# Another order of the calls on VectorE, GpSimd, ScalarE and TensorE in a two-layer recurrent block on one core

## The chip, the core and the metric

The kernel runs on one core of a Trainium2 chip, in one launch. The metric is the device time in microseconds (us). Every array is in HBM before the start and the output is there at the end.

## The reference

The input is 4 sequences of 1024 tokens with 256 channels, float32. Two layers follow each other, each with a sequence mixer and a feed-forward block; behind each of the four comes a residual sum and a layer norm.

```
x_conv = causal_depthwise_conv(x, 4 taps)                  # layer 0, mixer
r, i   = sigmoid(x_conv @ Wr.T + br), sigmoid(x_conv @ Wi.T + bi)
a      = sigmoid(log_a) ** (8 r);  b = sqrt(max(1 - a*a, 1e-6)) * (i * x_conv)
h      = scan along the tokens with a, b, its log clipped at -80
y0     = rmsnorm(h @ out_w.T) * norm_w
ffn    = relu(x @ W1 + b1) @ W2 + b2                       # 256 -> 1024 -> 256, in both layers
xz     = x @ in_proj.T;  xc = silu(conv4(x_in))            # layer 1, mixer (16 states per channel)
B, C, dt = parts of xc @ x_proj.T;  dt = softplus(dt * dt_w + dt_b)
h_n    = exp(dt * A_n) * h_n + dt * B_n * xc,  n = 0..15
y1     = (sum_n h_n * C_n) * silu(z) @ out_proj.T
```

## The kernel before

The 4096 tokens are cut into ten chunks (256, 256, 512 tokens; then 512 four times; 512, 384, 128), numbered 0 to 9. Channels lie on the partitions in two halves, so a full chunk is a tile of 128 x 1024. The chunks go through a software pipeline with five roles: in step i, `ahead` is chunk i+1 (its first convolution), `gate` chunk i (layer 0 mixer, first half of its feed-forward), `prep` chunk i-1 (rest of that feed-forward, input projection and convolution of layer 1), `scan` chunk i-2 (the 16 states) and `tail` chunk i-3 (output projection and feed-forward of layer 1). Each engine has its own list of calls for a step, in four variants: `opening` (steps -1 to 1), `entry` (steps 2 and 3), `step` (4 to 9) and `closing` (10 to 12). A list is written out, one call after the other, and an engine runs it strictly in this order; semaphores make it wait for the others. Nothing else sets the order. A chunk "closes" when it ends its sequence (2, 4, 6, 9) and "opens" when it begins one (0, 3, 5, 7).

The calls that the text speaks of, with the engine and the line of the profile:

- States of layer 1, for each n: TensorE spreads B and C over the partitions (`spread_B`, `spread_C`, L2037); ScalarE makes the decay (`state_decay`, L819); VectorE makes `state_input` (L1435, u times B in PSUM), two `state_scan` (L1450, one for each half; the old states come in as `carry` in chunks that don't open) and `state_output` (L1461, h times C in PSUM); GpSimd adds it up (`sum_states`, L385) and copies the last column (`save_carry`, L392), in chunks that don't close. A scan of state n waits for the copy of state n-2. TensorE's `spread_C(n)` waits for the first scan of n.
- Layer 0 mixer: TensorE `gate_mm` (L1907), ScalarE `gate_tanh`, `root_ln`, `root_exp`, VectorE `log_A` (L1356), `decay_steps` (L1362), `gate_input` (L1373), `scaled_input` (L1380) and `recurrence` (two scans, L1388, both operands in SBUF); then TensorE `out_proj0` (L1914, out_w), which waits for the recurrence and, since it shares PSUM with z, for both `z_silu` (L1406).
- Convolution of layer 1: ScalarE `mconv_tap` 1 to 3 (L781), each followed by GpSimd's `mconv_add` (L358); then VectorE `mconv_silu` (L1411).
- `dt_x` (L1423, VectorE, two operands in SBUF) makes u for the next chunk. `readout` (L1468) ends the states of `tail`. `row_stats` and `row_moments` (L1271, L1276) feed the layer norm of `gate`.

The wait of the two scans on the operand just written stands in `state_scan`:

```
dve.wait_ge(S["dBx_ready"], NS * c + n + 1)      # by state_input(n), same engine
dve.wait_ge(S["dA_ready"], UNITS * c + k + 1)
```

Of the kernel before, what the change touches and what calls it, by code (L numbers as in the profile page):

```python
# [95 lines left out]
def build(nc, xT, x, par, ffb, rows, gateT, outT, inT, xpT, opT, w1a, w2a, w1b, w2b, out):  # L96
    ctx = ExitStack()
    with ctx:
# [197 lines left out]
        def _(pool):  # L296
# [97 lines left out]
            def opening(ahead, gate, prep, scan, tail):  # L394
                if prep is not None:
                    row_scales(LN_PREP, prep)
                if gate is not None:
                    inv_rms(gate)
                    rms_residual(gate)
                    gate_scales(gate)  # L400
                    add_bias(LN_GATE, 0, x1, x1b, S["x1b_ready"], gate)
                if prep is not None:
                    save_carry(prep, 0)
                    save_carry(prep, 1)
                if ahead is not None:
                    conv_add(ahead, 1)
                if prep is not None:
                    sum_states(prep, 1)
                    save_carry(prep, 2)
                if ahead is not None:  # L410
                    conv_add(ahead, 2)
                if prep is not None:
                    sum_states(prep, 2)
                if ahead is not None:
                    conv_add(ahead, 3)
                if prep is not None:
                    save_carry(prep, 3)
# [3 lines left out]
            def entry(ahead, gate, prep, scan, tail):  # L421
# [3 lines left out]
                if tail is not None:  # L425
                    sum_states(tail, NS - 1)
                if prep is not None:
                    row_scales(LN_PREP, prep)
                if scan is not None:
                    if scan.i > 0:  # L430
                        save_carry(scan, 1)
                        sum_states(scan, 1)
                        save_carry(scan, 2)
                if tail is not None:
                    row_scales(LN_Y, tail)
                if scan is not None:
                    if scan.i > 0:
                        sum_states(scan, 2)
                        save_carry(scan, 3)
# [4 lines left out]
                if prep is not None:  # L444
                    mconv_add(prep, 1)
                    mconv_add(prep, 2)
# [3 lines left out]
                if prep is not None:  # L450
                    mconv_add(prep, 3)
                if scan is not None:
                    sum_states(scan, 6)
                if gate is not None:
                    inv_rms(gate)
                if scan is not None:
                    save_carry(scan, 6)
                    save_carry(scan, 7)
                if gate is not None:
                    rms_residual(gate)  # L460
                if scan is not None:
                    save_carry(scan, 8)
                    save_carry(scan, 9)
                    sum_states(scan, 7)
                if gate is not None:
                    gate_scales(gate)
                if scan is not None:
                    save_carry(scan, 10)
                    sum_states(scan, 8)
                    save_carry(scan, 11)  # L470
                if tail is not None:
                    add_bias(LN_Y, 1, x3, x3b, S["x3b_ready"], tail)
                if scan is not None:
# [2030 lines left out]
```

## Time and profile before

| | us |
|---|---|
| median of 3 runs (lowest to highest) | 961.77 (959.21 to 962.63) |
| the profiled execution | 961.2 |
| its span, first to last instruction | 959.4 |
| VectorE busy in it | 802.2 |
| TensorE busy | 796.9 |
| ScalarE busy | 671.6 |
| GpSimd busy | 561.4 |

The busy times are read against the span; the 1.8 us between span and time lie around it. Shares over the whole run hide that the pipeline fills and drains, so the stretches have to be read one by one.

### The profile page before, as it was taken

Reading aid. Unit: us, or ns where it says so; the run is one execution under the profiler, and the core shown is the slowest. Engines: PE = TensorE matmul, PEld = TensorE weight load, DVE = VectorE, ACT = ScalarE, POOL = GpSimd, SP = SyncE. Lnnn points to the kernel's source line nnn. Section 1 sums busy time; section 2 is a strip of 40 time slices with the busy share of each in tenths; the row PEclk is TensorE's granted clock in tenths of the full one; section 3 lists DMA queues with packets and bytes.
Section 4 is the critical chain, followed back from the end, with each engine's and each line's share of the span. In section 5 each row is a group of like instructions: output and inputs, shape, how many; then the busy total and the mean of one; then the engine's idle time right before and its main releaser. Section 6 shows DMA issues by size and latency. Waiting matters only on the chain. (4 is left out here: it accounts for less than half of the span.)

```text
span 959.4 us, 9608 instructions
## 1 busy us (share of the span) xinstructions
PE 796.9 (83%) x2802; PEld 528.2 (55%) x2802; DVE 802.2 (84%) x1013; ACT 671.6 (70%) x1345; POOL 561.4 (59%) x468
## 2 busy tenths in 40 slices
PE   2385867978987799999899999998998797787585
PEld 1264644736554556475647564756476546546464
DVE  5245566677799999999999999999999999989761
ACT  4347687588767865997699769876976685465452
POOL 0202457437836793789378937893776376565421
PEclk9597977989998889999999999999999799789597
DMA  9000000000100010001000100010000000000000
GB/s 315 12 23 22 23 1 22 1 1 0 56 1 0 1 42 13 0 1 59 8 1 1 60 1 0 1 46 0 1 1 27 1 1 1 23 0 1 22 1 22
DMA packets 10341, 19.49 MB, mean 20 GB/s; under 512 B 1457, under 2 KB 5297, under 8 KB 10289
## 3 DMA queue, kind: packets, MB, share of 16 engines
q1 hardware_dynamic: 10288, 18.88, 5.8%
q8 instruction: 22, 0.36, 0.2%
q14 instruction: 31, 0.25, 0.1%
HBM read 14.69 MB, written 4.19 MB: 20 GB/s over the span
## 5 line engine op out<-in xcount | busy, mean ns | idle before, releaser
L385 POOL TENSOR_TENSOR y<-y,hC 128x1024 f32<-128x1024 f32 (+3 forms) x140 | 280.1, 2001 | 77.3 <-DVE hC L1461 73.4
L1914 PE MATMUL pC<-w,hT 128*128 128x256 f32 x1024 | 232.4, 382 | 4.9 <-ACT hT L754 4.9
L819 ACT ACTIVATE dA<-dt,A_neg 128x512 f32<-128x512 f32 (+3 forms) x320 | 187.5, 630 | 54.3 <-DVE hs L1450 53.8
L1914 PEld LDWEIGHTS pC<-w,hT 128*128 128x128 f32 x1024 | 194.5, 191 | 36.7 <-issue 7.2
L1450 DVE TENSOR_TENSOR_SCAN hs<-dA,carry,pS 128x512 f32<-128x512 f32 (+3 forms) x192 | 193.4, 1008 | 18.1 <-ACT dA L819 10.4
L2037 PE MATMUL pS<-stack,sel 97*128 97x512 f32 (+3 forms) x320 | 148.0, 515 | 54.5 <-DVE hs L1450 54.0
L1435 DVE TENSOR_TENSOR pS<-u,pS 128x1024 f32<-128x1024 f32 (+3 forms) x160 | 159.8, 999 | 17.4 <-PE pS L2037 16.8
L1461 DVE TENSOR_TENSOR hC<-hs,pS 128x1024 f32<-128x1024 f32 (+3 forms) x160 | 157.5, 985 | 15.3 <-PE pS L2037 15.1
L1450 DVE TENSOR_TENSOR_SCAN hs<-dA,pS 128x512 f32<-128x512 f32 (+1 forms) x128 | 138.2, 1080 | 14.6 <-POOL carry L392 6.0
L754 ACT ACTIVATE hT<-pA,ffb_sb 128x512 f32<-128x512 f32 (+3 forms) x160 | 94.7, 599 | 59.2 <-PE pA L1907 58.9
L1907 PE MATMUL pA<-tg,w 128*128 128x512 f32 (+3 forms) x320 | 127.9, 538 | 7.7 <-ACT hT L754 6.3
L1907 PE MATMUL pA<-x1T,w 128*128 128x512 f32 (+3 forms) x320 | 126.4, 542 | 2.4 <-ACT x1T L746 2.3
L2037 PEld LDWEIGHTS pS<-stack,sel 97*128 97x128 f32 x320 | 63.4, 204 | 100.6 <-DVE hs L1450 76.3
L1907 PEld LDWEIGHTS pA<-tg,w 128*128 128x128 f32 x320 | 59.8, 204 | 59.3 <-issue 31.7
L1907 PEld LDWEIGHTS pA<-x1T,w 128*128 128x128 f32 x320 | 62.9, 208 | 50.7 <-issue 35.9
L325 POOL TENSOR_TENSOR ve<-row_ms,eps_rows 128x4 f32<-128x4 f32 (+3 forms) x30 | 10.1, 338 | 133.4 <-ACT x1T L727 67.3
L358 POOL TENSOR_TENSOR yg<-yg,v 128x1024 f32<-128x1024 f32 (+3 forms) x27 | 55.9, 2072 | 34.5 <-ACT v L781 34.4
L1907 PE MATMUL pA<-conv,gate_w 128*128 128x512 f32 (+3 forms) x160 | 62.5, 539 | 12.1 <-DVE conv L1328 11.6
L727 ACT ACTIVATE x1T<-x 128x256 f32<-128x256 f32 x32 | 13.1, 409 | 62.0 <-DVE x L1316 62.0
L348 POOL TENSOR_TENSOR conv<-conv,yg 128x1024 f32<-128x1024 f32 (+2 forms) x24 | 50.3, 2095 | 5.4 <-ACT yg L660 5.3
L1914 PE MATMUL pC<-out_w,st 128*128 128x256 f32 x128 | 36.5, 446 | 17.6 <-DVE st L1388 16.2
L1907 PEld LDWEIGHTS pA<-conv,gate_w 128*128 128x128 f32 x160 | 32.1, 211 | 34.0 <-issue 27.6
(120 smaller groups left out, 1101.5 us busy)
## 6 DMA issues: line engine op xcount, KB each, us to landing
xt<-xT SPq DMA_DIRECT2D x6, 515.0 KB, 4.7
xtok<-x SPq DMA_DIRECT2D x6, 512.0 KB, 5.3
out<-x3b SPq DMA_DIRECT2D x6, 512.0 KB, 2.9
w<-w1a SPq DMA_DIRECT2D x1, 1024.0 KB, 8.3
w<-w2a SPq DMA_DIRECT2D x1, 1024.0 KB, 10.4
w<-w1b SPq DMA_DIRECT2D x1, 1024.0 KB, 8.3
w<-w2b SPq DMA_DIRECT2D x1, 1024.0 KB, 9.9
xt<-xT SPq DMA_DIRECT2D x2, 259.0 KB, 7.8
```

The source lines that it names most:

```text
L348: nc.gpsimd.tensor_tensor(conv[:, :, 0:ch.T], conv[:, :, 0:ch.T], tap[:, :, 0:ch.T], ALU.add).then_inc(S["conv_sum"], 1)
L358: nc.gpsimd.tensor_tensor(cv[:, :, 0:ch.T], cv[:, :, 0:ch.T], v[:, :, 0:ch.T], ALU.add).then_inc(S["mconv_sum"], 1)
L385: nc.gpsimd.tensor_tensor(y[:, :, 0:ch.T], so_far, hC[:, n % CRING, :, 0:ch.T], ALU.add).then_inc(S["y_sum"], 1)
L727: nc.scalar.activation(unused[:, b, :], rows[:, b, :], ACT.Square, scale=D ** -0.5, accum_out=row_ms[n][:, b:b + 1]).then_inc(ms_row[n], 1)
L754: nc.scalar.activation(hT[:, f, 0:ch.T], pA[f % 2][:, 0:ch.T], ACT.Relu, bias=ffb_sb[:, layer, f:f + 1]).then_inc(done, 1)
L819: nc.scalar.activation(dA[:, k % ARING, 0:ch.T], dt[ch.side][:, h, 0:ch.T], ACT.Exp, scale=A_neg[:, h, n:n + 1]).then_inc(S["dA_ready"], 1)
L1435: V.tensor_tensor(inputs(n)[:, :, 0:ch.T], u[:, :, 0:ch.T], B_bank(n)[:, 0:ch.T].unsqueeze(1).to_broadcast([P, H, ch.T]), ALU.mult).then_i ...
L1450: V.tensor_tensor_scan(hs[:, n % HRING, h, 0:ch.T], dA[:, k % ARING, 0:ch.T], inputs(n)[:, h, 0:ch.T], 0.0 if ch.opens else carry[:, n, h: ...
L1461: V.tensor_tensor(hC[:, n % CRING, :, 0:ch.T], hs[:, n % HRING, :, 0:ch.T], C_bank(n)[:, 0:ch.T].unsqueeze(1).to_broadcast([P, H, ch.T]), ...
L1907: mm = nc.tensor.matmul(dst[:, 0:ch.T], w[:, k, lo:lo + dst.shape[0]], src(k)[:, 0:ch.T], start=k == 0, stop=k == H - 1)
L1914: mm = nc.tensor.matmul(dst[:, b * D:b * D + D], src(k, t0), w[:, k, :], start=k == 0, stop=k == nk - 1)
L2037: return nc.tensor.matmul(dst[:, 0:ch.T], sel[0:NXK, row:row + 1].to_broadcast([NXK, P]), stack[ch.side][0:NXK, 0:ch.T], start=True, stop= ...
```

## The change

All 17 lists of calls hold the same calls as before, with the same sizes, buffers and waits; the order within 16 of them is another (SyncE's is as it was). VectorE's, GpSimd's, ScalarE's and TensorE's lists for `opening`, `entry`, `step` and `closing` are rewritten; one move, `conv_early` in VectorE's `opening`, moves nothing, since it acts only in steps without a `prep`. The core of the diff, from GpSimd's `step`:

```
                     sum_states(scan, 5)
                     save_carry(scan, 5)
                 if prep is not None:
                     mconv_add(prep, 2)
+                    mconv_add(prep, 3)
                 if scan is not None:
                     sum_states(scan, 6)
                     save_carry(scan, 6)
-                if prep is not None:
-                    mconv_add(prep, 3)
+                    save_carry(scan, 7)
                 if gate is not None:
                     inv_rms(gate)
...
```

The change moves line numbers by 3 on VectorE (L1450 is L1453) and by 4 on TensorE (L2037 is L2041).

VectorE, `step` with chunk 3 in the role `scan`, states 6 to 8, before (hs is the scan, hC the output, pS the input, zz `z_silu`, tg `scaled_input`, st the recurrence):

```order
L1406 SCALAR_TENSOR_TENSOR zz<-zz,pC 128x512
L1450 SCALAR_TENSOR_TENSOR hs<-dA,pS 128x512
L1461 TENSOR_TENSOR hC<-hs,pS 128x1024
L1450 SCALAR_TENSOR_TENSOR hs<-dA,pS 128x512
L1435 TENSOR_TENSOR pS<-u,pS 128x1024
L1406 SCALAR_TENSOR_TENSOR zz<-zz,pC 128x512
L1380 SCALAR_TENSOR_TENSOR tg<-tg,inj 128x1024
L1388 SCALAR_TENSOR_TENSOR st<-decay,st,tg 128x512 x2
L1450 SCALAR_TENSOR_TENSOR hs<-dA,pS 128x512
```

and of the change:

```order
L1464 TENSOR_TENSOR hC<-hs,pS 128x1024
L1453 SCALAR_TENSOR_TENSOR hs<-dA,pS 128x512
L1409 SCALAR_TENSOR_TENSOR zz<-zz,pC 128x512 x2
L1383 SCALAR_TENSOR_TENSOR tg<-tg,inj 128x1024
L1438 TENSOR_TENSOR pS<-u,pS 128x1024
L1453 SCALAR_TENSOR_TENSOR hs<-dA,pS 128x512
L1391 SCALAR_TENSOR_TENSOR st<-decay,st,tg 128x512 x2
L1464 TENSOR_TENSOR hC<-hs,pS 128x1024
```

The state input of state 7 now stands directly ahead of the scan that reads it, where `z_silu` and `scaled_input` stood between them.

GpSimd, the same `step`, from `sum_states` 5 on (yg is `mconv_add`), before:

```order
L385 TENSOR_TENSOR y<-y,hC 128x1024
L392 COPY carry<-hs 128x2
L358 TENSOR_TENSOR yg<-yg,v 128x1024
L385 TENSOR_TENSOR y<-y,hC 128x1024
L392 COPY carry<-hs 128x2
L358 TENSOR_TENSOR yg<-yg,v 128x1024
```

and of the change:

```order
L385 TENSOR_TENSOR y<-y,hC 128x1024
L392 COPY carry<-hs 128x2
L358 TENSOR_TENSOR yg<-yg,v 128x1024 x2
L385 TENSOR_TENSOR y<-y,hC 128x1024
L392 COPY carry<-hs 128x2 x2
```

`mconv_add` 3 moved ahead of `sum_states` 6 and of the carry copy of state 6.

TensorE, first `entry` step (chunk 2 is `gate`, 1 `prep`, 0 `scan`), around `out_proj0` (out_w), before:

```order
L1907 MATMUL pA<-x1T,in_w 128x256 x2
L2037 MATMUL pS<-stack,sel 128x256 x2
L1907 MATMUL pA<-x1T,in_w 128x256 x2
L1907 MATMUL pC<-x1T,in_w 128x256 x4
L2037 MATMUL pS<-stack,sel 128x256 x3
L1914 MATMUL pC<-out_w,st 128x256 x8
```

and of the change:

```order
L1911 MATMUL pA<-x1T,in_w 128x256 x2
L2041 MATMUL pS<-stack,sel 128x256
L1911 MATMUL pA<-x1T,in_w 128x256 x2
L2041 MATMUL pS<-stack,sel 128x256 x2
L1911 MATMUL pC<-x1T,in_w 128x256 x2
L2041 MATMUL pS<-stack,sel 128x256
L1911 MATMUL pC<-x1T,in_w 128x256 x2
L2041 MATMUL pS<-stack,sel 128x256 x3
L1918 MATMUL pC<-out_w,st 128x256 x8
```

Two more `spread` matmuls, `spread_B(8)` and `spread_C(7)`, stand ahead of `out_proj0`; the second waits for the first scan of state 7.

## Rows read from the trace of the kernel before

**Rows 1.** The page, busy time of each engine over the whole run

```profile
PE 796.9 (83%) x2802; PEld 528.2 (55%) x2802; DVE 802.2 (84%) x1013; ACT 671.6 (70%) x1345; POOL 561.4 (59%) x468
```

**Rows 2.** Busy time by stretch; columns: stretch, length, then engines, TensorE clock, DMA

```profile
0.00:120.00 120.00, 68.88 (x244) 51.54 (x245) 58.52 (x152) 64.10 (x130) 26.60 (x44) 0.82 0.23 79
120.00:280.00 160.00, 134.01 (x464) 88.36 (x463) 118.30 (x176) 118.12 (x238) 92.92 (x94) 0.90 0.04 12
280.00:880.00 600.00, 539.85 (x1889) 347.48 (x1888) 583.07 (x602) 453.97 (x884) 413.68 (x295) 0.96 0.04 12
880.00:960.00 80.00, 54.12 (x210) 40.86 (x208) 42.31 (x87) 35.46 (x96) 28.23 (x36) 0.78 0.03 14
```

**Rows 3.** What VectorE waited for, 280 to 880 us: total, times, longest

```profile
DVE hs L1450 <- DVE pS L1435: 4.2, 21, 0.2
DVE pS L1435 <- PE pS L2037: 2.7, 6, 1.3
DVE hs L1450 <- POOL carry L392: 2.6, 4, 1.6
```

**Rows 4.** VectorE in order of time at two recurrences; columns: start, duration, instruction, [idle before <-releaser]

```profile
303.22 4.51 DVE L1388 TENSOR_TENSOR_SCAN st<-decay,st,tg 128x512 f32<-128x512 f32 x2
...
402.22 2.46 DVE L1388 TENSOR_TENSOR_SCAN st<-decay,st,tg 128x512 f32<-128x512 f32 x2
```

**Rows 5.** GpSimd in order of time beside them, and beside dt_x

```profile
303.79 2.85 POOL L358 TENSOR_TENSOR yg<-yg,v 128x1024 f32<-128x1024 f32 x1 [2.27 <-ACT v L781]
...
449.33 3.29 POOL L385 TENSOR_TENSOR y<-y,hC 128x1024 f32<-128x1024 f32 x1 [0.49 <-DVE hC L1461]
```

**Rows 6.** VectorE, a state_input and what follows it, chunks 3 and 2

```profile
430.86 1.21 DVE L1435 TENSOR_TENSOR pS<-u,pS 128x1024 f32<-128x1024 f32 x1
432.26 1.22 DVE L1450 TENSOR_TENSOR_SCAN hs<-dA,pS 128x512 f32<-128x512 f32 x1 [0.20 <-DVE pS L1435]
...
435.64 1.21 DVE L1435 TENSOR_TENSOR pS<-u,pS 128x1024 f32<-128x1024 f32 x1
436.76 0.68 DVE L1316 TENSOR_TENSOR x3b<-pC,x3b 128x512 f32<-128x512 f32 x1
...
289.05 1.21 DVE L1435 TENSOR_TENSOR pS<-u,pS 128x1024 f32<-128x1024 f32 x1
290.35 1.28 DVE L1450 TENSOR_TENSOR_SCAN hs<-dA,carry,pS 128x512 f32<-128x512 f32 x1
```

**Rows 7.** TensorE, out_proj0 of chunk 2 in the first entry step

```profile
130.60 3.78 PE L1914 MATMUL pC<-out_w,st 128*128 128x256 f32 x8
```

**Rows 8.** VectorE between the recurrence and state 7, first and second entry step

```profile
130.46 0.68 DVE L1461 TENSOR_TENSOR hC<-hs,pS 128x512 f32<-128x512 f32 x1
...
131.66 0.67 DVE L1435 TENSOR_TENSOR pS<-u,pS 128x512 f32<-128x512 f32 x1
134.48 0.69 DVE L1450 TENSOR_TENSOR_SCAN hs<-dA,pS 128x256 f32<-128x256 f32 x1 [2.15 <-POOL carry L392]
...
214.12 0.69 DVE L1406 SCALAR_TENSOR_TENSOR zz<-zz,pC 128x512 f32<-128x512 f32 x1 [1.48 <-ACT zz L786]
...
218.02 0.69 DVE L1461 TENSOR_TENSOR hC<-hs,pS 128x512 f32<-128x512 f32 x1 [2.36 <-PE pS L2037]
```

**Rows 9.** VectorE, dt_x in the opening, both entry steps and the closing step

```profile
87.00 0.66 DVE L1423 SCALAR_TENSOR_TENSOR u<-dt,v 128x512 f32<-128x512 f32 x1
...
167.25 1.44 DVE L1423 SCALAR_TENSOR_TENSOR u<-dt,v 128x512 f32<-128x512 f32 x1
...
252.42 1.80 DVE L1423 SCALAR_TENSOR_TENSOR u<-dt,v 128x1024 f32<-128x1024 f32 x1
...
888.15 1.76 DVE L1423 SCALAR_TENSOR_TENSOR u<-dt,v 128x256 f32<-128x256 f32 x1
```

**Rows 10.** VectorE's first scan of state 8 of chunk 3, and GpSimd's mconv_add(3)

```profile
409.52 1.22 DVE L1450 TENSOR_TENSOR_SCAN hs<-dA,pS 128x512 f32<-128x512 f32 x1 [0.36 <-POOL carry L392]
...
409.44 2.37 POOL L358 TENSOR_TENSOR yg<-yg,v 128x1024 f32<-128x1024 f32 x1
```

More of the change, by code:

```diff
@@ new lines, in entry @@
+                if gate is not None:
+                    relu(0, gate, 1)
+                    relu(0, gate, 2)
+                if ahead is not None:
+                    conv_tap(ahead, 2, prep)
+                if gate is not None:
+                    relu(0, gate, 3)
+                    relu(0, gate, 4)
+                    relu(0, gate, 5)
+                if tail is not None:
+                    row_squares(LN_OUT, tail, x3b, x3)
+                if scan is not None:
+                    state_decay(scan, 15)
@@ L941, in entry @@
                     mconv_first(prep, tail)
+                if tail is not None:
+                    relu(1, tail, 0, prep)
+                if prep is not None:
+                    mconv_tap(prep, 1)
+                if gate is not None:
+                    root_ln(gate)
+                if prep is not None:
+                    z_tanh(prep, 0)
+                    z_tanh(prep, 1)
+                if gate is not None:
+                    root_exp(gate)
+                if tail is not None:
+                    relu(1, tail, 1)
@@ new lines, in step @@
+                if scan is not None:
+                    state_decay(scan, 12)
+                    state_decay(scan, 13)
+                if gate is not None:
+                    relu(0, gate, 0, tail)
+                    relu(0, gate, 1)
+                if ahead is not None:
+                    conv_tap(ahead, 2, prep)
+                if scan is not None:
+                    state_decay(scan, 14)
+                if gate is not None:
+                    relu(0, gate, 2)
+                    relu(0, gate, 3)
@@ L1567, in entry @@
                 if tail is not None:
-                    add_ssm(tail, 0)
+                    readout(tail, gate)
                 if scan is not None:
@@ L1574, in entry @@
                         state_scan(scan, 3, 0)
+                        state_output(scan, 2)
+                if tail is not None:
+                    add_ssm(tail, 0)
+                if scan is not None:
+                    if scan.i > 0:
+                        state_scan(scan, 3, 1)
+                        state_input(scan, 4)
                 if gate is not None:
@@ new lines, in step @@
+                if tail is not None:
+                    if tail.nj == 2:
+                        add_ffn1(tail, 1)
+                if scan is not None:
+                    state_scan(scan, 14, 0)
+                    state_output(scan, 13)
+                    state_scan(scan, 14, 1)
+                    state_input(scan, 15)
+                    state_scan(scan, 15, 0)
+                    state_output(scan, 14)
+                if prep is not None:
+                    dt_x(prep)
+                    state_input(prep, 0)
@@ L2288, in step @@
                     up(1, tail, 0, prep)
+                if prep is not None:
+                    in_proj_z(prep, 0, tail)
                 if scan is not None:
```

1458 lines of the change are left out of this document (706 added, 752 removed).

## The prediction

> **What bounds the kernel now.** I read the page, then the busy times by stretch, then VectorE's waits, then the places where VectorE and GpSimd run side by side. The page shows VectorE busy 802.2 us and TensorE 796.9 of a span of 959.4 [rows 1]. That is two half-truths. By stretch, VectorE is busy 583 of the 600 us from 280 to 880, GpSimd only 414 and ScalarE 454 [rows 2]: there VectorE is the bound, and 16.9 us of idle time is all that any order can take out of it, apart from instructions that take too long. TensorE is busy 540 there, but no long wait of VectorE is on it: 2.7 us in all [rows 3]. Ahead of 280 us VectorE idles 103 us (61.5 and 41.7), behind 880 some 37 us [rows 2]: the pipeline fills and drains along chains through all engines, and an order can gain or lose whole microseconds.
>
> **What the change aims at.** A VectorE instruction with both operands in SBUF and a GpSimd instruction hold each other up. In one recurrence the two scans take 2.46 us (at 402.22 [rows 4]); in an earlier one 4.51, while GpSimd's `mconv_add` runs from 303.79 [rows 4, 5]. VectorE lost 2.05 us. In the other direction GpSimd's add takes 3.29 us beside `dt_x` [rows 5] instead of 2.37 [rows 10], and costs VectorE nothing. Among all such instructions of VectorE in its timeline only four are lengthened by more than 0.1 us: this one, and `dt_x` three times, 1.44 where 0.66 is due, 1.80 where twice 0.66 is, and 1.76 for half the size that takes 0.66 [rows 9], so 0.8, 0.5 and at least 1.1; the others already stand first. What the change is for is worth 2.05 + 0.8 + 0.5 + 1.1 = 4.4 us on the bounding engine, perhaps 4.8, and the two small ones lie in the entry steps, where VectorE has time. GpSimd's own losses don't matter to the end as long as it idles a third of the time [rows 2].
>
> By the Trainium skill ("SBUF — State Buffer", Who interferes with whom) whichever of the two starts first holds the shared interface for its whole instruction, and `tensor_scalar` in its fast mode contends too, also with one operand. The traces agree on the first part (4.51 for 2.46 where GpSimd was first, 3.29 for 2.37 where VectorE was); the second part is not looked at by the change, and no row here shows a case of it.
>
> **The sum**, against the profiled execution, 961.2 us (0.6 below the median of the three runs).
>
> 1. *Lock at 303 gone.* `scaled_input` and the recurrence stand two calls later, `mconv_tap` 1 and its add earlier: -2.05.
> 2. *Input directly ahead of its scan.* A scan that follows its `state_input` at once starts 1.40 us after it (430.86 to 432.26), where another instruction between starts after 1.12 (435.64 to 436.76): 0.28 us lost. With a carry it is 1.30 (289.05 to 290.35), 0.18 lost [rows 6]. In VectorE's `step` list I count 7 such neighbours before and 10 now, in `closing` 9 and 14. Six `step` steps, three of each kind: 3 x 3 x 0.28 + 3 x 3 x 0.18 = +4.1. One full closing step: 5 x 0.18 = +0.9. All of it lies in the stretch where VectorE is 97% busy, so it counts in full; nothing covers it. The page already holds 4.2 us of this wait [rows 3].
> 3. *Opening.* `dt_x` (0.66 us [rows 9]) goes ahead of `row_moments`, which the chain of the gate chunk through GpSimd, ScalarE and TensorE waits for: +0.7.
> 4. *First entry step.* `out_proj0` started at 130.60 [rows 7], with state 6 not begun to be read out. Now it stands behind `spread_C(7)`: VectorE must first do an output, a scan, an input and the first scan of state 7: 0.68 + 0.69 + 0.67 + 0.69 [rows 8], +2.7. The 2.15 us that the last one waited for the carry copy [rows 8] should go, since the copy of state 5 now stands ahead of `mconv_add` 2. If it doesn't go, the term is +4.9.
> 5. *Second entry step.* VectorE waited 1.48 us for `z_tanh` and 2.36 for `spread_C(5)`, which stood behind five `up` [rows 8]. `z_tanh` now stands ahead of a `state_decay` and the spread ahead of `in_proj_z`: -3.5, between -3.8 and 0.
> 6. *Carry of state 6.* It now stands behind `mconv_add` 3 on GpSimd. In chunk 3 the scan of state 8 already waited 0.36 us for that copy, and the add that now comes first took 2.37 us [rows 10]; `mconv_tap` 3 comes earlier by two calls. Only chunks 3, 5 and 7 copy. I take 0.5 each, nearer to the 0.36 that is there than to the add, +1.5; bounds -1.1 and +7.1.
> 7. *`dt_x` in the closing step* took at least 1.1 us too long [rows 9]. Now it stands behind `state_output(14)` and starts with GpSimd's add rather than into it; but the second `add_ffn1` comes ahead of a scan that covered its matmuls. Half: -0.6, between -1.3 and 0.
>
> Sum: -2.05 + 4.1 + 0.9 + 0.7 + 2.7 - 3.5 + 1.5 - 0.6 = **+3.8**, so **965 us**. `readout` and `seed_x3` earlier or later, `row_moments` directly behind `row_stats`, and the order of `add_ssm` go together at nothing: VectorE's work stays, and their partners have slack. The last step, chunk 9's way out through `tail`, has the same calls in the same order on every engine.
>
> For term 2 the Trainium skill says otherwise ("VectorE: DVE Perf Modes", The DRAIN you can't avoid): a chain of VectorE instructions takes the same time with a semaphore after each as without, the semaphore costs nothing. By it terms 2 would be nothing and the sum -1.2, 960 us. The pitches of 1.40 and 1.12 us in rows 6 speak against that here, and I go by them.
>
> **Rivals.**
> - *Faster: the new order also closes VectorE's other gaps.* For it: it reorders the feeders too, and the waits on spreads and carry copies from 280 to 880 hold 5.3 us [rows 3], the locks 4.8, the second entry step 3.8. All gone without the losses of terms 4 and 6, and term 2 at its 5.0: 961.2 - 5.3 - 4.8 - 3.8 + 5.0 + 0.7 = 953. Against it: those waits are spread thin, 0.2 to 1.6 us each, and every move opens others. 22%.
> - *Slower: `mconv_add` 2 now runs into the recurrence in every step.* `root_exp` stands ahead of `mconv_tap` 2 by one `relu`, `state_input` 7 and a scan stand between `scaled_input` and the recurrence: the add may start 1 to 2 us ahead of the recurrence, which then waits, up to the 2.05 us of rows 4. At 1.4 us in six steps this is +8.4, with the carries of term 6 late: 961.2 + 3.8 + 8.4 = 973. It decides once the tap ends before VectorE reaches the first scan of state 7. 20%.
> - *Nothing: the waits of term 2 are swallowed,* since VectorE stops at each step's boundary for the others anyway (and the skill's rule comes out the same way). 961.2 + 3.8 - 5.0 = 960. 16%.
> - The forecast: 42%, 960 to 970, three fifths of it within 0.5% of the median.
>
> **How the numbers follow.** 0.5% of 961.8 is 4.8 us, about what a measurement of this kernel can tell from no change: below 957.0 is faster, above 966.6 slower. Faster: the first rival, 0.22 with its edges. Same: 0.25 of the forecast and the third rival, 0.41. Slower: 0.17 and 0.20, 0.37. The range 950 to 976 reaches from the faster rival with 3 us beyond to the slower one with 3 us beyond; the unknown bounds of terms 4 and 6 (+2.2, +5.6) lie inside it.
>
> **What would show it.** Right: the VectorE wait of the scan on its input grows from 4.2 us to about 8; the recurrence row of chunk 4's step is 2.46; `out_proj0` of the first entry step starts near 134; in the second the waits of rows 8 are gone; chunks 3, 5 and 7 show a carry wait at state 8. Wrong: if VectorE's busy time from 280 to 880 falls by more than the locks, I miscounted them; if a recurrence takes over 3 us in most steps, the slower rival holds; if the stretch before 280 moves by more than 3 us, terms 3 to 5 are mis-sized, whatever the total.

## The result, and the profile after

The changed kernel takes 966.13 us (median of five runs, 965.11 to 966.78), the kernel before 961.77 beside it. The ratio is 1.0047, 95% interval 1.0031 to 1.0063. That is 1.1 us above the forecast of 965 and inside the range: 4.4 us slower, less than the 4.8 that the prediction counted as no change, and a sum of terms of both signs, as it had said. The page of the changed kernel, to be held against [rows 1]:

```profile
PE 789.9 (82%) x2802; PEld 523.7 (54%) x2802; DVE 801.2 (83%) x1013; ACT 673.9 (70%) x1345; POOL 554.6 (57%) x468
```

VectorE's busy time fell by only 1.0 us over the run. By stretch (same columns as [rows 2]) it fell by 3.8 from 280 to 880:

```profile
280.00:880.00 600.00, 532.73 (x1871) 342.06 (x1870) 579.24 (x595) 453.46 (x879) 406.90 (x294) 0.96 0.04 12
```

That is less work in the same window, since the pipeline runs later (595 instructions against 602). Between the same instructions, from the start of chunk 2's step to the end of chunk 7's, VectorE is busy 550.8 us before and 551.1 after, although a lock of 2.1 us is gone there: by rows 6 a scan directly behind its input gives up 0.09 us of overlap besides its wait. What the change aimed at is plain in single rows. In order of time, VectorE at the recurrences of chunks 2 and 3 in the role `scan`, and `dt_x` at the three places of [rows 9] where it took 1.44, 1.80 and 1.76 us:

```profile
401.16 1.22 DVE L1453 TENSOR_TENSOR_SCAN hs<-dA,pS 128x512 f32<-128x512 f32 x1 [0.65 <-ACT dA L821]
402.30 2.43 DVE L1391 TENSOR_TENSOR_SCAN st<-decay,st,tg 128x512 f32<-128x512 f32 x2
...
305.14 2.44 DVE L1391 TENSOR_TENSOR_SCAN st<-decay,st,tg 128x512 f32<-128x512 f32 x2
...
173.66 0.69 DVE L1426 SCALAR_TENSOR_TENSOR u<-dt,v 128x512 f32<-128x512 f32 x1
255.36 1.22 DVE L1426 SCALAR_TENSOR_TENSOR u<-dt,v 128x1024 f32<-128x1024 f32 x1
895.66 0.42 DVE L1426 SCALAR_TENSOR_TENSOR u<-dt,v 128x256 f32<-128x256 f32 x1
```

All four locks that the prediction listed are gone: 4.51 became 2.44, and 0.75, 0.58 and 1.34 us went at `dt_x`. That is 4.7 us. But a new one came in the second entry step, at a copy of six columns with one operand in SBUF, which starts behind GpSimd's add and ends with it. GpSimd, then VectorE:

```profile
174.99 2.37 POOL L348 TENSOR_TENSOR conv<-conv,yg 128x1024 f32<-128x1024 f32 x1 [6.47 <-ACT yg L662]
175.58 1.80 DVE L1405 COPY xi<-xi 128x6 f32<-128x6 f32 x1
```

The same copy took 0.17 us there in the kernel before, and 0.97 at 106.97, beside an add too. So a VectorE instruction with one operand can be held as well; the prediction had looked only at those with two. What this lock costs was not tried. What came instead shows in VectorE's waits from 280 to 880 (against [rows 3]):

```profile
DVE hs L1453 <- POOL carry L392: 5.9, 10, 1.3
DVE hs L1453 <- DVE pS L1438: 5.0, 25, 0.2
DVE hs L1453 <- ACT dA L821: 2.5, 7, 0.7
DVE zz L1409 <- ACT zz L788: 1.7, 3, 0.8
```

The wait for carry copies grew from 2.6 to 5.9, that of a scan on its own input from 4.2 to 5.0, that for ScalarE's decays from 1.9 to 2.5 and that for `z_tanh` from 0.4 to 1.7. The waits of 2.7 us on TensorE's spreads (pS) are no longer among the rows.

The time is best read step by step. The table cuts the run where VectorE starts `state_input(0)` of the next chunk, the first input behind each `dt_x`; lengths in us, each from one profiled execution. The first row begins with the span, the last ends with VectorE's last instruction. The four right columns are kernels of the experiments.

| from cut to cut | before | after | x_step | x_entry | z_carry | best |
|---|---|---|---|---|---|---|
| opening | 87.7 | 88.1 | 88.8 | 88.2 | 87.9 | 87.8 |
| first entry | 83.1 | 86.3 | 83.1 | 86.8 | 86.2 | 86.3 |
| second entry | 85.0 | 82.2 | 85.1 | 82.1 | 82.2 | 82.2 |
| chunk 2 | 99.0 | 95.8 | 96.8 | 97.8 | 95.8 | 95.6 |
| chunk 3 | 95.7 | 98.6 | 98.6 | 95.7 | 97.6 | 97.5 |
| chunk 4 | 95.8 | 96.4 | 96.5 | 95.9 | 96.4 | 96.5 |
| chunk 5 | 94.7 | 98.0 | 98.1 | 94.7 | 95.9 | 95.9 |
| chunk 6 | 93.3 | 93.6 | 93.6 | 94.2 | 93.6 | 93.6 |
| chunk 7 | 88.4 | 87.4 | 87.5 | 88.0 | 88.6 | 86.7 |
| closing, chunk 8 | 69.1 | 69.6 | 69.3 | 69.4 | 68.3 | 69.6 |
| chunk 9 to the end | 63.5 | 64.8 | 65.4 | 63.2 | 64.7 | 62.7 |

### The profile page after: what moved, and what is told of

Same layout as the page of the kernel before. It is cut to its first block and busy times, and to the rows that moved or that the text cites. A ratio compares the mean times of both kernels' runs of the same rounds, so it can differ in the third digit from the quotient of the medians.

```text
span 965.0 us, 9608 instructions
## 1 busy us (share of the span) xinstructions
PE 789.9 (82%) x2802; PEld 523.7 (54%) x2802; DVE 801.2 (83%) x1013; ACT 673.9 (70%) x1345; POOL 554.6 (57%) x468
## 5 line engine op out<-in xcount | busy, mean ns | idle before, releaser
L2041 PE MATMUL pS<-stack,sel 97*128 97x512 f32 (+3 forms) x320 | 161.5, 544 | 60.3 <-DVE hs L1453 60.0
L1453 DVE TENSOR_TENSOR_SCAN hs<-dA,carry,pS 128x512 f32<-128x512 f32 (+3 forms) x192 | 193.6, 1009 | 17.4 <-ACT dA L821 6.4
L1453 DVE TENSOR_TENSOR_SCAN hs<-dA,pS 128x512 f32<-128x512 f32 (+1 forms) x128 | 138.2, 1081 | 23.2 <-ACT dA L821 10.2
L2041 PEld LDWEIGHTS pS<-stack,sel 97*128 97x128 f32 x320 | 62.6, 203 | 110.8 <-DVE hs L1453 85.0
L325 POOL TENSOR_TENSOR ve<-row_ms,eps_rows 128x4 f32<-128x4 f32 (+3 forms) x30 | 6.0, 201 | 135.3 <-ACT x1T L729 84.3
L358 POOL TENSOR_TENSOR yg<-yg,v 128x1024 f32<-128x1024 f32 (+3 forms) x27 | 58.4, 2162 | 28.8 <-ACT v L783 28.8
L1929 PE MATMUL pA<-ident,x 128*128 128x128 f32 x128 | 22.3, 306 | 29.4 <-ACT x L720 16.4
L1918 PE MATMUL pC<-out_w,st 128*128 128x256 f32 x128 | 33.8, 420 | 15.2 <-DVE st L1391 13.3
```

Source lines behind the costliest of these rows:

```text
L358: nc.gpsimd.tensor_tensor(cv[:, :, 0:ch.T], cv[:, :, 0:ch.T], v[:, :, 0:ch.T], ALU.add).then_inc(S["mconv_sum"], 1)
L1453: V.tensor_tensor_scan(hs[:, n % HRING, h, 0:ch.T], dA[:, k % ARING, 0:ch.T], inputs(n)[:, h, 0:ch.T], 0.0 if ch.opens else carry[:, n, h: ...
L1918: mm = nc.tensor.matmul(dst[:, b * D:b * D + D], src(k, t0), w[:, k, :], start=k == 0, stop=k == nk - 1)
L1929: mm = nc.tensor.transpose(dst[:, b * P:b * P + P], x_[:, b, h * P:h * P + P], ident[:])
L2041: return nc.tensor.matmul(dst[:, 0:ch.T], sel[0:NXK, row:row + 1].to_broadcast([NXK, P]), stack[ch.side][0:NXK, 0:ch.T], start=True, stop= ...
```

## The experiments

**Which part of the change does what: x_step and x_entry.** Whole lists are taken from the changed kernel, on all four engines; the others stay as before.

```
x_step:  def step(...)                       from the changed kernel
x_entry: def opening(...), def entry(...)    from the changed kernel
```

> The kernel before with only the four `step` lists of the change (chunks 2 to 7 in the role scan); opening, entry and closing stay as before. Cut at VectorE's state_input(0) of the next chunk, the changed kernel took, against before, -3.2, +2.9, +0.6, +3.3, +0.3 and -0.9 us in these six steps, +3.0 in all. Theory A (the parts add up; each step loses or wins by its own order): 961.8 + 3.0 = 965 us, and the same signs step by step, above all chunks 3 and 5 about 3 us longer. Rival B (the long steps of chunks 3 and 5 only hand on what the entry steps did before them): 961 to 962, and chunks 3 and 5 within 1 us of before.

> The kernel before with only the opening and entry lists of the change on all four engines. The changed kernel took +0.4, +3.2 and -2.7 us there against before, and 3.2 less in the step of chunk 2, which follows. Theory A (what an entry step loses stays lost): +0.9, 962.7 us, with out_proj0 of the first entry step near 134.7 instead of 130.6. Rival B (chunk 2's gain of 3.2 us comes from how the entry ends, not from its own list): 959.5. A gain or loss under 1 us says that terms 3, 4 and 5 of the prediction cancel.

Measured: x_step 967.96 us beside 962.54 for the kernel before, ratio 1.0057 (1.0040 to 1.0073); x_entry 962.13, ratio 0.9997 (0.9988 to 1.0006). Theory A holds by signs and steps in both. In x_step chunks 3 to 7 are within 0.1 us of the changed kernel's, though opening and entry run the lists of before. Its total is 3 us above the 965 of theory A; in its profiled execution the opening was 1.1 us longer than before and the end 1.9, where its lists are the old ones. In x_entry the two entry steps are near the changed kernel's, +3.8 and -2.8 us (there +3.2 and -2.8). Chunk 2's gain of 3.2 comes from both, 2.2 from its own list and 1.2 from the entry. So the parts add, and the loss lies in `step`: its six steps are 4.2 us longer in x_step, while opening, entry and chunk 2 of x_entry give +0.3 together. The `closing` lists were not tried alone. In x_entry the recurrence of chunk 2 is still locked, in x_step it is not:

```profile
306.50 2.44 DVE L1384 TENSOR_TENSOR_SCAN st<-decay,st,tg 128x512 f32<-128x512 f32 x2
```

**What a direct neighbour costs: x_direct5 and x_cycle.** Both edit only VectorE's `step` of the kernel before.

```
 x_direct5, at states 3, 6, 10, 11 and 13 (here 3):
-state_input(scan, 3)
 readout(tail, gate)
+state_input(scan, 3)
 state_scan(scan, 3, 0)
 x_cycle, states 12 to 15 (here 13):
-state_scan(scan, 13, 0)
 state_output(scan, 12)
+state_scan(scan, 13, 0)
 state_scan(scan, 13, 1)
 state_input(scan, 14)
```

> The kernel before with five more places in VectorE's `step` list where a state_input stands directly ahead of the scan that reads it: readout, z_silu(0), row_stats, add_ffn1(0) and add_ffn1(1) go from between input and scan of states 3, 6, 10, 11 and 13 to ahead of the input. Theory A (the wait on the instruction just before costs 0.28 us of pitch without a carry and 0.18 with one, by rows 6): 6 steps x 5 places x 0.18 to 0.28 = 5.4 to 8.4 us, so 967.2 to 970.2, and the VectorE wait on its own input grows from 21 times to 36 in the three chunks that show it. Rival B (the wait costs nothing, as the skill's rule has it, or is swallowed elsewhere): 961.8, within 1 us.

> The kernel before with states 12 to 15 in VectorE's `step` list in another cycle: both scans of n, input of n+1, output of n, so that no instruction reads what the one directly before it wrote; three direct neighbours (states 12 to 15, less the one that add_ffn1 parts) go in each of six steps. Theory A: 6 x 3 x 0.18 to 0.28 = 3.2 to 5.0 us less, 957 to 958.6, if TensorE spreads C in the 2.4 us that are left between first scan and output. Rival B: the spread of C comes late, VectorE waits for TensorE up to 1 us at each of three outputs, and the kernel is 5 to 18 us slower. Rival C: the neighbours cost nothing, no change.

x_direct5 takes 971.59 us, ratio 1.0099 (1.0086 to 1.0112), 9.0 us more. VectorE's waits from 280 to 880:

```profile
DVE hs L1450 <- DVE pS L1435: 6.2, 31, 0.2
DVE zz L1406 <- ACT zz L786: 3.9, 4, 1.4
```

The wait is charged to the input 31 times, not 36, since in some rows another releaser is named with the same 0.20 us:

```profile
434.40 1.21 DVE L1435 TENSOR_TENSOR pS<-u,pS 128x1024 f32<-128x1024 f32 x1
435.81 1.22 DVE L1450 TENSOR_TENSOR_SCAN hs<-dA,pS 128x512 f32<-128x512 f32 x1 [0.20 <-ACT dA L819]
```

By start times it is exact: summed over a step, the pitches are 1.43 to 1.45 us longer in chunks 3, 5 and 7 (0.29 each for five places) and 0.71 to 0.93 in 2, 4 and 6 (0.18 each, for four places in chunk 2 and five in the others), 6.9 us in all. The profiled steps grew by 7.7: `z_silu(0)`, one call earlier, also waits for `z_tanh` now, 3.5 us more than before, and other waits closed by 2.7. Of the six steps it does so in those of chunks 3, 6 and 7 only, where TensorE was granted 0.50 for a stretch, and not in 4 and 5, where it had 1.00 throughout. The price of term 2 is confirmed. The Trainium skill ("VectorE: DVE Perf Modes", The DRAIN you can't avoid) says that the semaphore cost nothing in its chain of copies; that doesn't describe these pairs.

What decides between the two prices isn't the carry, as the prediction and the expectations have it, but the number of waits ahead of the scan. `state_scan` waits for `carry_saved` besides its input and decay if the chunk doesn't close and n is 2 or more, or if it doesn't open and n is below 2. The kernel before has every mix. State 1 of chunk 2 (carry, extra wait), state 1 of chunk 3 (no carry, no extra wait), and a state of chunk 8 (carry, extra wait, 384 columns):

```profile
263.14 1.23 DVE L1435 TENSOR_TENSOR pS<-u,pS 128x1024 f32<-128x1024 f32 x1 [1.29 <-PE pS L2037]
264.57 1.28 DVE L1450 TENSOR_TENSOR_SCAN hs<-dA,carry,pS 128x512 f32<-128x512 f32 x1 [0.20 <-DVE pS L1435]
...
361.72 1.23 DVE L1435 TENSOR_TENSOR pS<-u,pS 128x1024 f32<-128x1024 f32 x1 [1.26 <-PE pS L2037]
363.04 1.22 DVE L1450 TENSOR_TENSOR_SCAN hs<-dA,pS 128x512 f32<-128x512 f32 x1
...
841.27 0.94 DVE L1435 TENSOR_TENSOR pS<-u,pS 128x768 f32<-128x768 f32 x1
842.41 1.01 DVE L1450 TENSOR_TENSOR_SCAN hs<-dA,carry,pS 128x384 f32<-128x384 f32 x1 [0.20 <-DVE pS L1435]
```

The pitches are 1.43, 1.32 and 1.14 us, the last against 0.85 with another instruction between: 0.31, 0.20 and 0.29 lost. In all fourteen traces a direct pair that waits for nothing longer (a gap under 0.3 us) has 0.20 us or a little more with the extra wait, carry or not, and without it 0.09 or less in all but nine of 522 places. No run changed the wait itself.

x_cycle removes direct neighbours, two a step and not the three that were counted, and still takes 964.90, ratio 1.0035 (1.0021 to 1.0048). None of its theories had the reason. TensorE was in time; the pitches fell by 0.3 to 0.6 us a step, 0.18 or 0.29 for each of the two. But `dt_x` came to stand beside GpSimd's adds: it had started as `state_output(14)` ended, 0.2 us ahead of the sum that waits for that output, and now a scan stands between the two. By form, x_cycle:

```profile
L1423 DVE SCALAR_TENSOR_TENSOR u<-dt,v 128x1024 f32<-128x1024 f32 x6 | 13.6, 2270 | 0.1
L1423 DVE SCALAR_TENSOR_TENSOR u<-dt,v 128x768 f32<-128x768 f32 x1 | 2.6, 2595 | 0.0
```

In the kernel before the six took 7.9 us and the one of 768 columns 0.95. Locks of 7.4 us ate the gain.

**Undoing terms 6 and 2 in the changed kernel: y_carry, y_apart, y_all.**

```
 y_carry, GpSimd step:             y_apart, VectorE step:
 mconv_add(prep, 2)                 decay_steps: between input and scan 4
-mconv_add(prep, 3)                 gate_input:  between input and scan 5
 sum_states(scan, 6)                scaled_input: between input and scan 7
 save_carry(scan, 6)               y_all: both, and on ScalarE
+mconv_add(prep, 3)                 state_decay(7) ahead of mconv_tap(2)
```

> The changed kernel with GpSimd's mconv_add(3) put back behind sum_states(6) and save_carry(6) in `step`. In the changed kernel the first scan of state 8 waited 1.28, 1.29 and 0.74 us for that carry copy in chunks 3, 5 and 7, before the change 0.36, 0.36 and 1.61. Theory A (term 6: the position on GpSimd makes this wait): in chunks 3 and 5 it falls to 0.4 or less, the two steps take 0.9 us less each, the kernel 1 to 2 us less, 964 to 965. Rival B (the add now comes late instead, mconv_silu waits for it): the two steps as long as they were, 966.

> The changed kernel with three places of VectorE's `step` list parted again: decay_steps between input and scan of state 4, gate_input at state 5, scaled_input at state 7. Nothing else. Theory A (term 2): each of the six steps takes 3 x 0.28 (chunks 3, 5, 7) or 3 x 0.18 us (2, 4, 6) less, 4.1 us in all, 962.0 for the kernel. Rival B (the waits on other engines take the place, since VectorE arrives earlier): under 1.5 us gained, and the waits for carry, decay and z_tanh in chunks 3 and 5 grow by what is gained.

> The changed kernel with both edits above and ScalarE's state_decay(7) ahead of mconv_tap(2), for which the first scan of state 7 waited 0.65 us in chunks 3 and 5 (behind two calls that stand ahead of it since the change). If the three costs are separate, they add: 4.1 + 1.5 + 1.3 = 6.9 us less than the changed kernel, 959.2, which is below the kernel before. If VectorE's waits only hand the time on, 962 to 964.

All three missed by far: 980.26, 979.98 and 998.54 us, ratios to the kernel before 1.0207 (1.0182 to 1.0232), 1.0199 (1.0180 to 1.0218) and 1.0393 (1.0372 to 1.0413). In y_carry the carry wait falls as wished, but `sum_states(6)` must wait for `state_output(6)`, and `mconv_add` 3 behind it starts at 411.02 where it had started at 403.85. The waits of y_carry from 280 to 880, VectorE's and then ScalarE's:

```profile
DVE v L1416 <- ACT v L797: 12.3, 6, 2.2
```

```profile
ACT v L797 <- POOL yg L358: 29.9, 6, 5.6
```

VectorE waits 2.2 us in nearly every step at `mconv_silu`, which the change had moved ahead of `state_output(7)`. Before, the add was as late (409.44 [rows 10]) and `mconv_silu` stood two calls later. GpSimd's and VectorE's moves belong together.

In y_apart the pitches do get shorter, by 0.18 or 0.29 us a place, but `decay_steps` comes three calls later, and ScalarE stands still at `decays`, for which it never waits from 280 to 880 in the changed kernel:

```profile
ACT decay L694 <- DVE decay L1365: 14.0, 6, 3.9
```

Everything behind it on ScalarE is late, and VectorE waits for decays and `z_tanh` in its turn.

y_all shows the rival of the slower side as a mechanism. Its recurrences of 512 columns, and those of the changed kernel:

```profile
L1393 DVE TENSOR_TENSOR_SCAN st<-decay,st,tg 128x512 f32<-128x512 f32 x12 | 22.9, 1944 | 0.2
```

```profile
L1391 DVE TENSOR_TENSOR_SCAN st<-decay,st,tg 128x512 f32<-128x512 f32 x12 | 14.7, 1262 | 0.2
```

The recurrence is now locked in every step, as in chunk 3, where GpSimd's add starts at 408.39 and VectorE's pair at 408.42:

```profile
408.42 4.57 DVE L1393 TENSOR_TENSOR_SCAN st<-decay,st,tg 128x512 f32<-128x512 f32 x2
```

```profile
408.39 2.35 POOL L358 TENSOR_TENSOR yg<-yg,v 128x1024 f32<-128x1024 f32 x1 [3.91 <-ACT v L785]
```

Three hundredths of a microsecond decide over 2.1 us. The locks are 1.5 to 2.2 us a step; the wait at `mconv_silu`, up to 2.2 us as in y_carry, and waits for `z_tanh` and TensorE's spreads make up the rest.

**Parting three pairs in the kernel before: y_sep.**

```
 a2_minus_1 -> between input and scan 4    mconv_silu -> between input and scan 9
 decay_steps -> ... 5                      row_moments -> ... 11, add_ffn1(0) -> ... 12
```

> The kernel before with three more inputs parted from their scans in VectorE's `step` list: a2_minus_1 at state 4 so that decay_steps can go to state 5, mconv_silu at state 9, row_moments at state 11 so that add_ffn1(0) can go to state 12. Theory A: 6 steps x 3 places at 0.28 or 0.18 us, 4.1 us less, 957.7. Rival B (the later calls make ScalarE or TensorE late, which VectorE waits for in its turn: decay_steps, mconv_silu and row_moments come 1 to 4 us later): new waits of 0.5 us and more at x_proj_low, at the recurrence or at the next chunk's inputs, and 961 to 965.

1008.59 us, ratio 1.0492 (1.0477 to 1.0507). Rival B, far larger than put: ScalarE waits for `decay_steps` in each step, 5.8 us at the longest, and VectorE then 28 us for spreads.

```profile
ACT decay L692 <- DVE decay L1362: 32.6, 6, 5.8
```

```profile
DVE hC L1461 <- PE pS L2041: 15.5, 6, 3.2
DVE pS L1435 <- PE pS L2041: 12.7, 11, 3.1
```

**The same undoings with nobody waiting: z_carry and z_pairs.** Both start from the changed kernel.

```
 z_carry, GpSimd step:         z_pairs, VectorE step:
 mconv_add(prep, 2)             gate_input:  between input and scan 5
+save_carry(scan, 6)            scaled_input: between input and scan 7
 mconv_add(prep, 3)
 sum_states(scan, 6)
-save_carry(scan, 6)
```

> The changed kernel with only GpSimd's save_carry(6) (0.19 us) put between mconv_add(2) and mconv_add(3) in `step`, where GpSimd stood idle 1.51 us in chunk 3; sum_states(6) stays behind. Putting that sum back too had made mconv_add(3), mconv_tanh and so VectorE's mconv_silu 2.3 us late. Theory A: the wait of state 8 on the copy (1.28 and 1.29 us in chunks 3 and 5) falls to 0.2, mconv_silu waits for nothing, the two steps are 1.0 us shorter each, the kernel 964 to 965. Rival B: ScalarE is what paces this part of the step, VectorE then waits 1 us more for mconv_tanh, and the time is that of the changed kernel.

> The changed kernel with two inputs parted from their scans by calls that no other engine waits for before the recurrence: gate_input goes between input and scan of state 5, scaled_input between those of state 7; decay_steps stays, since moving it had made ScalarE wait 1.6 us at each step's decays. Theory A (0.28 without, 0.18 with a carry): 6 steps, 2 x 0.28 or 2 x 0.18, 2.8 us less than the changed kernel, 963.4, half of a per cent of it in chunks 3 and 5. Rival B (VectorE arrives earlier and waits for ScalarE's z_tanh and state_decay instead): direct neighbours 11 to 9 in each step, but the waits on ScalarE grow by the same 0.4 to 0.6 us, and no time is gained in the steps of chunks 3 and 5.

z_carry takes 961.71 us beside 962.17, ratio 0.9998 (0.9987 to 1.0009): 4.4 us less than the changed kernel, for another place of a copy of 0.19 us. VectorE's first scan of state 8 in chunk 3 now waits 0.20 instead of 1.28, and GpSimd beside it:

```profile
408.11 1.22 DVE L1455 TENSOR_TENSOR_SCAN hs<-dA,pS 128x512 f32<-128x512 f32 x1 [0.20 <-DVE pS L1440]
```

```profile
402.10 0.19 POOL L392 COPY carry<-hs 128x2 f32<-128x2 f32 x1
403.67 3.04 POOL L358 TENSOR_TENSOR yg<-yg,v 128x1024 f32<-128x1024 f32 x1 [1.38 <-ACT v L785]
```

The table gives -1.0 in chunk 3, -2.1 in 5, +1.2 in 7 and -1.3 in the closing step. Theory A holds for chunks 3 and 5, where all behind that scan comes 1.07 and 1.09 us earlier. The other half of chunk 5's gain is there ahead of it, and TensorE's clock makes it. The same four matmuls of in_w, and the stretch they lie in (columns as [rows 2]), in the changed kernel and in z_carry:

```profile
575.83 3.67 PE L1911 MATMUL pA<-x1T,in_w 128*128 128x512 f32 x4 [1.10 <-ACT x1T L748]
...
575.83:579.50 3.67, 3.67 (x5) 1.60 (x6) 3.47 (x4) 3.67 (x7) 3.48 (x4) 0.54 0.00 0
```

```profile
574.59 1.98 PE L1913 MATMUL pA<-x1T,in_w 128*128 128x512 f32 x4 [1.10 <-ACT x1T L750]
...
574.59:576.57 1.98, 1.98 (x5) 0.86 (x5) 1.78 (x2) 1.98 (x4) 1.98 (x2) 1.00 0.00 0
```

In the changed kernel they ran at a mean clock of 0.54, from 576.0 us on at 0.50 (1.2 GHz). ScalarE was late behind them, and VectorE waited 0.48 us for `z_tanh`, 0.22 at `scaled_input` and 0.26 more for a decay; in z_carry they ran at 1.00 (2.4 GHz), the first two waits are gone and all comes 1.06 us earlier. The kernel before had 1.00 there too. Chunk 3 has such a stretch at 381.4 us in the changed kernel, at the same place of its step in x_step, z_carry and best, and none before. Chunk 7's +1.2 is one that z_carry has and the changed kernel doesn't: the sixteen matmuls of the output projection come late, VectorE waits 1.59 us for them, and the carry gives back 0.5. So of the 4.4 us the copy accounts for some 2.2 in chunks 3 and 5 and 0.5 in chunk 7. The closing step was not taken apart.

z_pairs takes 970.41, ratio 1.0090 (1.0074 to 1.0107). Chunks 3 and 5 are 0.8 us shorter than in the changed kernel, where A had 0.56, but that is the clock: z_pairs was granted 1.00 throughout both. Against z_op0 below, which has the changed kernel's `step` lists and 1.00 there too (97.6 and 97.0 us), they are 0.3 longer, with recurrences 0.3 too long and waits for the decay of state 7 0.2 longer. So the edit gained nothing in any step, and rival B is nearer. Chunk 2 lost 2.4. `scaled_input` started 0.50 us ahead of GpSimd's add in the changed kernel; now it starts 1.03 behind it, and both it and the recurrence are locked:

```profile
301.95 2.42 DVE L1383 SCALAR_TENSOR_TENSOR tg<-tg,inj 128x1024 f32<-128x1024 f32 x1
...
305.48 3.93 DVE L1391 TENSOR_TENSOR_SCAN st<-decay,st,tg 128x512 f32<-128x512 f32 x2
```

```profile
300.92 2.36 POOL L358 TENSOR_TENSOR yg<-yg,v 128x1024 f32<-128x1024 f32 x1
```

Chunk 7 lost 3.2 more: 2.5 in instructions that took longer, above all `scaled_input` of 256 columns (1.53 us, against 0.78) and the recurrence of twice 128 (2.44, against 0.84), and 1.5 in two waits for TensorE's output projection that the changed kernel doesn't have and z_op0 and z_carry have, behind a stretch at 0.50; other waits shrank.

**Undoing term 4: z_op0.** The changed kernel, `entry` only.

```
 VectorE:                      TensorE:
 state_scan(scan, 6, 0)         spread_C(scan, 6)
+z_silu(prep, 0 and 1)         +out_proj0(gate, prep)
 ...                            spread_B(scan, 8)
-z_silu(prep, 0)                up(1, tail, 4)
 state_scan(scan, 7, 0)         spread_C(scan, 7)
-z_silu(prep, 1)               -out_proj0(gate, prep)
```

> The changed kernel with term 4 undone in `entry`: z_silu(0) and (1) directly behind the first scan of state 6, out_proj0 directly behind spread_C(6). Theory A (term 4): out_proj0 of the first entry step starts at 132.3 instead of 134.75, row_stats comes 2.4 us earlier, and the first entry step is 2 to 2.5 us shorter, 964. Rival B (the step's end is set by ScalarE's list, where state_decay(15) now stands behind row_squares and a relu: VectorE waited 4.6 us for it at 170.7): row_stats earlier, but the end of the step within 0.5 us of the changed kernel, and that wait grows.

968.05 us, ratio 1.0058 (1.0043 to 1.0074). `out_proj0` of the first entry step started at 132.11 instead of 134.75 and `row_stats` 1.6 us earlier, and yet the step is only 0.4 shorter (85.9): rival B. The second entry step became 3.2 us longer (85.4), back at its length before the change, with the wait of [rows 8] for `z_tanh` back, 1.32 us:

```profile
215.67 0.69 DVE L1409 SCALAR_TENSOR_TENSOR zz<-zz,pC 128x512 f32<-128x512 f32 x1 [1.32 <-ACT zz L788]
```

ScalarE's list is the changed one here, and `z_tanh` as early in the step as there. So the second step gains by the later place of `z_silu` on VectorE, or of `out_proj0` that moves with it, the same edit that term 4 charges in the first. Chunks 3 and 5 became 1.04 and 1.07 us shorter with unchanged `step` lists, since their stretches at 0.50 were gone, and chunk 4, which got one, 0.93 longer.

**All that helped: best.** z_carry, `gate_input` alone between input and scan of state 5, and in ScalarE's `entry`:

```
 relu(0, gate, 3)
+state_decay(scan, 15)
 relu(0, gate, 4)
 relu(0, gate, 5)
 row_squares(LN_OUT, tail, x3b, x3)
-state_decay(scan, 15)
```

> The changed kernel with three edits: save_carry(6) between the two adds (alone it brought the kernel from 966.1 to 961.7 us); gate_input between input and scan of state 5 in `step`; and in ScalarE's `entry` state_decay(15) ahead of relu(4) instead of behind relu(5) and row_squares. Theory A for the last: the first entry step is long because VectorE waits 4.61 us at 170.7 for that decay, which stands behind relus that TensorE feeds every 1.72 us; two of them less is 3.4 us, so the wait falls to about 1.2, the step is 2.5 to 3.5 us shorter, and the second entry step, where no such wait stood, keeps its length. Rival B: TensorE's spread (1.65 us of wait behind it) or the next step takes the time back, under 1 us gained. For gate_input: one direct neighbour less in each of six steps, 0.28 us in chunks 3, 5, 7 and 0.18 in 2, 4, 6, 1.4 us in all, if scaled_input still starts ahead of GpSimd's add in chunk 2's step (0.5 us ahead in the changed kernel); if not, a lock of 1.2 to 2.4 us comes back there, as with two places parted. Together 961.7 - 3 - 1.4 = 957 us, below both kernels; with the rival and the lock 962.

960.32 us beside 961.32, ratio 0.9994 (0.9984 to 1.0004): not told apart from the kernel before, and 0.5% below the changed one (0.9994 against 1.0047), but not the 957 of theory A. No recurrence and no `dt_x` is locked; the copy of six columns still takes 1.81 us at 175.28. Moving the decay gained nothing: the first entry step stays at 86.3. VectorE at its end, in the changed kernel and here:

```profile
170.72 0.69 DVE L1453 TENSOR_TENSOR_SCAN hs<-dA,pS 128x256 f32<-128x256 f32 x1 [4.61 <-ACT dA L821]
173.06 0.69 DVE L1464 TENSOR_TENSOR hC<-hs,pS 128x512 f32<-128x512 f32 x1 [1.65 <-PE pS L2041]
```

```profile
166.98 0.69 DVE L1456 TENSOR_TENSOR_SCAN hs<-dA,pS 128x256 f32<-128x256 f32 x1 [1.18 <-ACT dA L823]
172.75 0.69 DVE L1467 TENSOR_TENSOR hC<-hs,pS 128x512 f32<-128x512 f32 x1 [5.08 <-PE pS L2044]
```

The wait for the decay fell by 3.4 us and the next one, for TensorE's spread behind the `up` matmuls, grew by 3.4. TensorE sets this end, as rival B had it. `gate_input` gained 0.2 us in chunk 2 and nothing in the others: the pitch is 0.18 or 0.29 us shorter, but `gate_input` itself now takes 0.1 to 0.2 us longer beside GpSimd's sum in four of the steps, and decays are waited for a little longer.

## Why the prediction was right, point by point

- **Term 1, the lock (-2.05): right.** 4.51 to 2.44 us, with the `step` lists alone (x_step).
- **Term 2, direct neighbours (+4.1 and +0.9): the price was right in the steps, the sum too high.** 0.29 and 0.18 us for each (x_direct5). The places grew by three a step as counted, and by five in the closing step. But in the chunks that open, up to four of these pairs also wait for a copy or a decay, so that the 0.2 us is inside a longer wait: counted by the pairs that wait for nothing longer, the six steps lost 2.0 us by it, not 4.1. The row of VectorE's waits grew to 5.0 us, not to 8, and could not have reached 8: the gap of 0.09 us in chunks 2, 4 and 6 is too short to be listed, so nine new places of 0.20 are the most that it can show. Chunks 4 and 6, where the only longer new wait is one of 0.40 and 0.23 us for a decay, grew by 0.6 and 0.3, for a forecast of 0.54 each. In the closing step the price was wrong, 0.29 each (rows of chunk 8 above) and not 0.18, so 1.45 for 0.9; it came out at +0.5 with term 7 in it, forecast +0.3.
- **Term 3, opening (+0.7): can't be told.** +0.4, while x_step, which leaves the opening as it was, shows +1.1.
- **Term 4, first entry step (+2.7): the size was near, the cause was wrong.** The carry wait of 2.15 us at state 7 went, but one of 3.15 came at state 4. `out_proj0` started at 134.75, near the 134 that was named, and the step grew by 3.2. But 1.6 us of the delay was there at the recurrence (128.50 for 126.86 before): ScalarE's sums for `prep` had waited 6.3 us for a residual, 4.1 before. And z_op0 gave 2.6 us back at `out_proj0` for 0.4 at the end. The price was charged one for one along a chain whose end TensorE sets.
- **Term 5, second entry step (-3.5): the size near, the cause incomplete.** -2.8, with a lock of 0.6 gone and one of 1.6 new. z_op0 takes it back whole, although `z_tanh` stays early: without the edit that term 4 priced as a pure loss there is no gain.
- **Term 6, carry of state 6 (+1.5): the mechanism right, its size not the whole of it.** The waits at state 8 went from 0.36, 0.36 and 1.61 to 1.28, 1.29 and 0.74, +1.0 in sum and a gain in chunk 7 that I hadn't seen. Chunks 3 and 5 lost 2.9 and 3.3 us, for which terms 2 and 6 had 1.3. About 1.07 us in each is the carry (z_carry). About 1.05 in each is TensorE at 0.50 (z_op0, z_carry), which shows as 0.45 and 0.48 us at `z_tanh` and 0.22 at `scaled_input`; no term had it. The rest, 0.8 and 1.2 us, holds what is left of the wait for the decay of state 7 (0.65, of which some 0.25 go with the clock), which ScalarE now issues behind `mconv_tap` 2, and in chunk 3 0.78 for a copy at state 15. The prediction named decays in no term.
- **Term 7, `dt_x` in the closing step (-0.6):** 1.34 us gone, the bound, not half of it.
- **What "goes together at nothing"** was wrong in chunk 2: -3.2 for a forecast of -1.5. There a wait of 0.92 us for the spread of state 7 went, one of 1.19 for a decay became one of 0.84 for a copy, and one of 1.29 for the spread of state 1 fell to 0.67. x_entry, with the old `step` lists, shows all three, so the way the entry ends is enough for them; why the first is gone in x_step too was not found. In chunk 3 the new `step` lists took away a wait of 1.26 (1.26 still in x_entry, none in x_step).
- **The end (0): +1.2.** x_step, whose `closing` lists are the old ones, shows +1.9 there; it is a matter of TensorE's clock, below.

The sum of the terms was +3.8, of the measured parts +5.6 in the profiled executions and +4.4 by medians. It was right by luck, because over- and undersized terms cancelled: too much for term 2, nothing for ScalarE's decays and nothing for the clock, which has some 2.1 us in chunks 3 and 5 and about 1 at the end. Whether the new order brings these stretches at 0.50 or they fell so is open. The faster rival didn't come: the waits on spreads closed and others opened. The slower rival's mechanism is real (y_all, z_pairs) but missed the changed kernel by half a microsecond or less.

## What to carry to other kernels

Where four engines run fixed lists, a list is a piece of one schedule. Moves that took away a visible cost lost 14 to 47 us here against the kernel that they started from, because calls on other engines had been placed for the old order; before moving an instruction, ask of each engine who waits for it, and move only what nobody waits for, like the 0.19 us copy that gave 1.07 us back in each of two steps. Gains against locks hang on start times that differ by 0.03 to 0.5 us: any edit that shifts VectorE by that much, even a faster one, has to be read again for locks, one-operand copies included. A difference of 1 us in one step is put to an edit only when TensorE's clock in that step is the same in both traces; the 0.8 us of z_pairs in chunks 3 and 5 were the clock's. And cut both traces at one instruction of each step before naming causes: the table told more than any total.

## What the runs showed of the hardware

The last stretch, chunk 9 to the end, has the same order of calls in z_carry and best, and TensorE's clock made it 2.0 us longer in one. Stretch, length, then busy times and the granted clock as in [rows 2], z_carry then best:

```profile
892.55:957.23 64.68, 49.36 (x183) 37.42 (x183) 31.36 (x74) 27.61 (x76) 19.69 (x26) 0.76 0.04 14
```

```profile
891.67:954.34 62.67, 47.49 (x183) 36.12 (x183) 31.34 (x74) 27.62 (x76) 19.70 (x26) 0.80 0.04 15
```

The same 183 matmuls, 49.4 us at a mean of 0.76 and 47.5 at 0.80; the other engines' work is equal to 0.02 us. The two levels of 1.2 and 2.4 GHz (0.50 and 1.00) are both in the stretch, in other shares. The changed kernel's end is of the longer kind (49.44 us of matmuls in 64.76 us at 0.76). With the old `closing` lists the kernel before has 47.66 in 63.53 at 0.77 and x_step 49.84 in 65.40 at 0.76; so 0.01 of the mean does not tell them apart, and it matters which matmuls ran at 0.50. Together with the steps above, where one stretch at 0.50 made 0.9 to 1.7 us, 1 to 2 us of any comparison of single steps or ends here can be the clock's.

In z_op0 it shows at the start of the `up` matmuls of the first entry step. TensorE had been granted 0.50 (1.2 GHz) through the transposes ahead of them in both kernels; then, the first twelve of these matmuls in order of time, and the stretch they lie in, for z_op0 and for the changed kernel:

```profile
156.19 7.20 PE L1909 MATMUL pA<-x1T,w 128*128 128x512 f32 x12 [0.25 <-ACT x1T L748]
...
156.19:163.40 7.21, 7.21 (x14) 3.22 (x15) 3.14 (x5) 4.33 (x7) 5.54 (x5) 0.75 0.00 0
```

```profile
157.81 6.27 PE L1911 MATMUL pA<-x1T,w 128*128 128x512 f32 x12 [0.25 <-ACT x1T L748]
...
157.81:164.00 6.19, 6.19 (x13) 2.82 (x14) 3.14 (x5) 4.32 (x7) 5.55 (x5) 0.86 0.00 0
```

z_op0 reached them 1.6 us earlier and was 0.9 us slower in them, at a mean clock of 0.75 for 0.86: a chain that gains time in front of TensorE can lose it again to the clock.
